# A sequence layer with ten dense experts on 8 cores: half of the pre-pass products on GpSimd, small filler matmuls, and other slots for the weights

## The reference, cut to what matters

```python
x = x + attn(layernorm(x))          # attn: state-space scan, then a 1024-4096-1024 MLP
x = x + ffn(layernorm(x))           # ffn: 2 shared experts and 8 routed ones
...
def step(s, u_t):                   # scan over time, 1024 channels x 16 states
    s = s * dA + u_t[..., None] * dB
    y = jnp.einsum('bdn,dn->bd', s, C_ssm)
    return (s, y)
...
h = gelu(rmsnorm(x) @ w1 + b1) @ w2 + b2
...
h_s = experts(u, W1_s, W2_s).sum(-2)            # every token, 2 experts
scores = sigmoid(u @ centroids); top 2 of 8
h_r = sum of gk * experts(u, W1_r, W2_r) over the top 2
return u + h_s + h_r
```

## Time and profile before

| what | us |
|---|---|
| two executions | 7874.85 and 8011.66 |
| their median | 7943.26 |
| the profiled execution, its own time | 7874.85 |
| span of its slowest core (core 1), the one shown | 7872.9 |
| spans of all cores | 7825.0 to 7872.9 |
| start and first load | 0 to 87 |
| pre-pass | 87 to 592 |
| scan | 592 to 2105 |
| MLP | 2105 to 2660 |
| router | 2660 to 2900 |
| experts and output | 2900 to 7873 |

### The profile page before, as it was taken

The page is one execution under the profiler, slowest core; times in us unless marked ns, Lnnn a source line. Parts: engine busy times, 40 slices in busy tenths (PEclk is TensorE's granted clock), DMA queues, the critical chain, the costliest instruction groups (busy, mean ns, idle before and its releaser), DMA issues.

```text
span 7872.9 us, 63136 instructions; the slowest of 8 cores (7825.0 to 7872.9 us)
## 1 busy us (share of the span) xinstructions
PE 5210.4 (66%) x23040; PEld 2278.9 (29%) x23040; DVE 2353.5 (30%) x2813; ACT 1454.9 (18%) x2046; POOL 1666.4 (21%) x1608
## 2 busy tenths in 40 slices
PE   0000000000288527999999999999999999999998
PEld 0000000000133213444434444444444444444443
DVE  5889898989611350000000000000000000000001
ACT  5780000000111002211122111222111221111220
POOL 0007786967300001101111111111011111111110
PEclk5555555555699768999999999999999999999997
DMA  3100000000133105555555555555555555555553
GB/s 94 27 0 0 6 0 6 0 8 0 14 46 50 23 11 89 70 67 70 74 87 73 67 70 75 68 74 67 70 70 75 72 71 68 70 71 73 70 73 78
DMA packets 555731, 412.68 MB, mean 52 GB/s; under 512 B 13194, under 2 KB 546586, under 8 KB 553764
## 3 DMA queue, kind: packets, MB, share of 16 engines
q0 software_dynamic: 545280, 381.73, 36.3%
q1 hardware_dynamic: 7844, 18.54, 0.7%
q10 hardware_dynamic: 2304, 8.39, 0.3%
HBM read 765.12 MB, written 12.58 MB: 99 GB/s over the span
## 4 chain that ended last, share of the span: by engine, by line
PE 60%; issue 13%; DVE 13%; DMA 7%; POOL 5%; ACT 2%; DVEq 0%; POOLq 0%; SPq 0%; ACTq 0%
PE ps L939 29%; PE ps L900 23%; POOL SSb L266 5%; DMA STAT<-W1r 4%; PE ps L710 3%; DVE SSb L554 3%; PE ps L668 3%; DVE BIG L269 2%; DVE BIG L266 2%; DVE MXS L269 1%; DVE MXS L266 1%; PE ps L991 1%; DMA STAT<-W1s 1%; DMA WBUF<-W1r 1%; POOL SSb L273 1%
## 5 line engine op out<-in xcount | busy, mean ns | idle before, releaser
L939 PE MATMUL ps<-WBUF,XR 128*128 128x512 bf16 x10240 | 2262.2, 384 | 131.9 <-DVE BIG L269 111.4
L276 ACT ACTIVATE XR<-ps,BIA 128x512 bf16<-128x512 f32 x1280 | 879.4, 687 | 3791.0 <-PE ps L900 3791.0
L939 PEld LDWEIGHTS ps<-WBUF,XR 128*128 128x128 bf16 x10240 | 1010.1, 99 | 1384.1 <-issue 211.1
L269 DVE SCALAR_TENSOR_TENSOR BIG<-ps,WTOK,BIG 128x512 f32<-128x512 f32 x256 | 171.5, 744 | 3657.9 <-PE ps L939 3657.9
L900 PE MATMUL ps<-MXS,WBUF 128*128 128x512 bf16 x5120 | 1140.4, 380 | 95.2 <-DVE MXS L262 38.2
L900 PE MATMUL ps<-MXS,STAT 128*128 128x512 bf16 x5120 | 1137.3, 380 | 76.0 <-DMA STAT<-W1r 58.7
L419 PE MATMUL ps<-BIG,ONE 128*128 128x512 bf16 x32 | 13.9, 614 | 1432.1 <-ACT BIG L276 1432.1
L554 DVE TENSOR_TENSOR_SCAN SSb<-COEF,SSb,BIG 128x512 f32<-128x512 f32 x512 | 879.8, 1756 | 0.0
L900 PEld LDWEIGHTS ps<-MXS,WBUF 128*128 128x128 bf16 x5120 | 493.8, 98 | 729.8 <-issue 160.5
L900 PEld LDWEIGHTS ps<-MXS,STAT 128*128 128x128 bf16 x5120 | 494.2, 98 | 708.8 <-issue 137.5
L280 POOL DMA_DIRECT2D WBUF<-W2r x256 | 190.0, 746 | 1656.7 <-PE ps L939 1589.2
(11 more groups left out here) (88 smaller groups left out, 1820.6 us busy)
## 6 DMA issues: line engine op xcount, KB each, us to landing
WBUF<-W2r POOLq DMA_DIRECT2D x256, 512.0 KB, 5.5
WBUF<-W1r POOLq DMA_DIRECT2D x128, 512.0 KB, 6.2
STAT<-W1r POOLq DMA_DIRECT2D x128, 512.0 KB, 6.3
WBUF<-W2s POOLq DMA_DIRECT2D x64, 512.0 KB, 6.5
WBUF<-w POOLq DMA_DIRECT2D x40, 512.0 KB, 5.9
WBUF<-W1s POOLq DMA_DIRECT2D x32, 512.0 KB, 6.2
STAT<-W1s POOLq DMA_DIRECT2D x32, 512.0 KB, 6.4
XR<-x SPq DMA_DIRECT2D x1, 8192.0 KB, 35.9
```

Source lines behind the costliest of these rows:

```text
L269: return lambda e: e.scalar_tensor_tensor(out, in0, s, in1, op0, op1, accum_out=acc)
L276: return lambda e: e.activation(out, in0, fn, bias=bias, scale=scale, accum_out=acc)
L939: last = e.matmul(ps[tgl * 2 + ti][:, 0:TT], haps[ti][:, tgl * 128:(tgl + 1) * 128], w2t, start=(hsub == 0), stop=(hsub == NH - 1))
```

## The change

It does five things.

1. In the pre-pass the even gn stay as they were. For the odd gn POOL multiplies the weight row with the input into `prod_p` (one buffer of 512 columns, region `ss_tmp`, the same columns as `tmp_p`), and DVE sums `prod_p` by a `tensor_scalar` with an accumulator output.
2. `pe_warm` puts a matmul of 128x128x128 of ones into ps3 on PE's list, after every even gn in the pre-pass and in the scan (64 a tile, 512 in all). It waits for the DVE instruction emitted last, and nothing waits for it.
3. The two W1 slots are now both in STAT (columns 0 to 1023 and 1024 to 2047), and W2 has four slots in WBUF, `% 4`. `w2slot2` is defined and not used.
4. The load of the first w1 chunk in advance is gone; it is emitted at the start of the MLP like the others.
5. The router's bf16 tile names one more region of WBUF among its writes.

```diff
+        def pe_warm():
+            b.plan["t"].append((
+                [("v", b.cnt["v"])],
+                lambda e: e.matmul(ps[3][:, 0:128], ONE[:, :], ONE[:, :],
+                                   start=True, stop=True), None, 0))
...
-        w1slot = [(WBUF[:, 3072:4096].bitcast(BF16), [wb_w1[1]]),
-                  (STAT[:, 0:1024].bitcast(BF16), [st_rg[0], st_rg[1]])]
+        w1slot = [(STAT[:, 0:1024].bitcast(BF16), [st_rg[0], st_rg[1]]),
+                  (STAT[:, 1024:2048].bitcast(BF16), [st_rg[2], st_rg[3]])]
         w2slot = [(WBUF[:, i * 1024:(i + 1) * 1024].bitcast(BF16),
-                   [[wb_w2[0], wb_w2[1], wb_w1[0]][i]])
-                  for i in range(3)]
+                   [[wb_w2[0], wb_w2[1], wb_w1[0], wb_w1[1]][i]])
+                  for i in range(4)]
...
+            prod_p = SSb[:, 4 * TT + 2 * GN:5 * TT + 2 * GN]
             for gn in range(GN):
...
-                b.op("v", STT(MXS[:, dumpo:dumpo + TT], ew, 1.0,
-                              up_ap[:, g * TT:(g + 1) * TT], ALU.mult,
-                              ALU.mult, acc=smp_ap[:, gn:gn + 1]),
-                     reads=[expw_rg[esl], up_rgs[g]],
-                     writes=dump_rg + [smp_rg[pt]])
+                if gn % 2 == 0:
+                    b.op("v", STT(MXS[:, dumpo:dumpo + TT], ew, 1.0,
+                                  up_ap[:, g * TT:(g + 1) * TT], ALU.mult,
+                                  ALU.mult, acc=smp_ap[:, gn:gn + 1]),
+                         reads=[expw_rg[esl], up_rgs[g]],
+                         writes=dump_rg + [smp_rg[pt]])
+                else:
+                    b.op("p", TTo(prod_p, ew, up_ap[:, g * TT:(g + 1) * TT],
+                                  ALU.mult),
+                         reads=[expw_rg[esl], up_rgs[g]], writes=[ss_tmp])
+                    b.op("v", TSc(MXS[:, dumpo:dumpo + TT], prod_p, 1.0,
+                                  None, ALU.mult, ALU.add,
+                                  acc=smp_ap[:, gn:gn + 1]),
+                         reads=[ss_tmp],
+                         writes=dump_rg + [smp_rg[pt]])
+                if gn % 2 == 0:
+                    pe_warm()
...
+                if gn % 2 == 0:
+                    pe_warm()
...
-            if t == NT - 2:
-                w1c0, w1rgs0 = w1slot[0]
-                b.dma("qg", DMA(w1c0.rearrange("p (dg h) -> p dg h", h=256),
...
-                if not (q == 0 and hc == 0):
...
-                        psl = (hsub // 4) % 3
+                        psl = (hsub // 4) % 4
...
-        xbf4_rgs = [wb_w2[0], wb_w2[1], wb_w1[0]]
+        xbf4_rgs = [wb_w2[0], wb_w2[1], wb_w1[0], wb_w1[1]]
...
-                    psl = (hsub // 4) % 3
+                    psl = (hsub // 4) % 4
```

More of the change, by code:

```diff
@@ L652, in build_program @@
                 h0 = q * QH + hc * 256
[L653 to L658 removed]
+                src = dr["w1"][:, h0:h0 + 256].rearrange(
+                    "(dg p) h -> p dg h", p=128)
+                b.dma("qg", DMA(w1c.rearrange("p (dg h) -> p dg h", h=256),
+                                src), writes=w1rgs)
                 for hs in range(2):
```

10 lines of the change are left out of this document (2 added, 8 removed).

## The result

| | us |
|---|---|
| changed kernel, 14 executions: median (lowest to highest) | 8722.64 (8277.31 to 8954.89) |
| kernel before in the same job, 12 executions | 8002.21 (7842.88 to 8772.06) |
| ratio of the counted executions | 1.0562 [1.0464, 1.0660] |
| the same two kernels on another chip, medians of all executions | 8261.43 against 7883.75 |
| ratio of the counted executions there | 1.0473 [1.0421, 1.0526] |

What is left to explain is a ratio of 1.047 to 1.056 where 1.044 was forecast.

The account below looks back on a forecast made before the run. The prediction took DVE to bound the first 2.1 ms (pre-pass and scan) and PE the rest. 7874.85 + 284 (loop) + 62 (tile changes) = 8221 us, +4.4%, range 8120 to 8310.

Parts of the forecast that it names:

- The ring of sum, multiply and product: Pre-pass loop: one product buffer makes sum, multiply and product follow one another, 2.72 us a pair against 1.61, +284 us.
- a bound at +26 us: Pre-pass loop: POOL-to-DVE hand-overs of 0.2 us in place of the assumed 0.1 would add 26 us.
- That product and multiply exclude each other: Pre-pass loop: POOL's product and DVE's even multiply do not overlap; the product ends 1.11 us after the multiply.
- beside the even multiply: Rival, pre-pass loop: the product overlaps the even multiply, pair 2.25 us, +164 us, total 8101 us; chance 0.08.
- The sum is the long form: Pre-pass loop: DVE's sum with accumulator takes 0.69 us; the short form, 0.43, would give back 67 us.
- Between the tiles: Four tile changes: the next load now stands behind the products, +15.4 us each, +62 us in all.
- Item 2, on the path up to the experts: 0: Small matmuls in pre-pass and scan cost 0; without the late load, each tile change would be 4.5 us longer.
- the rival asked for a lifted clock: Rival, pre-pass and scan: small matmuls raise PE's clock, saving 28 us and 2 at the MLP's start, total 8191; chance 0.06.
- Item 3 at 0: Experts: the new weight slots gain nothing, since PE waits for no W2 load and W1 keeps two slots.
- its bound of -72: Experts: -72 us if all of PE's waits for W1 loads, 58.7 and 13.4 us, went.
- Items 4 and 5 at 0: MLP start: the second W1 chunk still arrives some 23 us early, and the added wait is for finished readers; 0.
- the slowest core moves with the rest: Whole kernel: terms added to the profiled execution's 7874.85 us, with everything behind the pre-pass shifted and of the same length.

Follow-up runs that it names:

- one_input: `split_hoist` with the even gn on DVE as a one-operand sum of the weight row, input product left out; one execution, cores 7989 to 8011 us.
- scan_dve: Kernel before with the scan's odd-gn multiply and add moved from POOL to DVE; median 8134.27 us, lowest 7669.93, no ratio.
- two_buf: `split_hoist` with two product buffers in turn instead of one; 7926.08 us in the counted execution of two.
- split_hoist: Kernel before plus item 1, with the next tile's bf16 load issued ahead of the products; 8398.86 us, ratio 1.0367 [1.0033, 1.0701].
- split_only: Kernel before plus item 1 alone (odd products on POOL, one product buffer); 8264.86 us, ratio 1.0431 [1.0230, 1.0633].
- warm_dense: `warm_only` with 12 small matmuls in place of one at every even gn; 7893.28 us in the counted execution of two.
- warm_only: Kernel before plus item 2 alone, the 512 small matmuls in pre-pass and scan; 8205.24 us, no counted execution, no ratio.
- slots_only: Kernel before plus items 3, 4 and 5 alone (weight slots, no load in advance); 7964.69 us, ratio 0.9996 [0.9938, 1.0055].
- best: Kernel before with items 3, 4 and 5, the scan without POOL, and the scan of gn + 1 emitted ahead; 7573.86 us, ratio 0.9607 [0.9583, 0.9631].
- after_again: The changed kernel, unaltered, run again on the same chip as `nowarm`; 8261.43 us, ratio 1.0473.
- nowarm: Changed kernel without its 512 small matmuls (item 2 undone); single counted execution 8231.56 us, 1.045 over the kernel before's mean, no interval.
- warm_pre: Kernel before plus the 256 small matmuls of the pre-pass only; ratio 1.0162 [1.0097, 1.0228].
- warm_scan: Kernel before plus the 256 small matmuls of the scan only; ratio 1.0062 [1.0028, 1.0097].

## Why the prediction was wrong by its number and right about the pre-pass

**The ring of sum, multiply and product: right, its hand-over too short.** Forecast 0.81 + 0.69 + 1.11 + 0.10, measured 0.80 + 0.69 + 1.13 + 0.20. The hand-over was taken from gaps of 0.14 and 0.17 less "a little other work"; it is 0.20, the value that the prediction kept as a bound at +26 us. With 2.81 for 2.72 the loop costs 307 instead of 284. That product and multiply exclude each other was an inference from six lengths of the earlier trace rows; `one_input` shows it (with the open end named there), `scan_dve` shows it from the other side, and `two_buf` shows that the loss needed the one buffer as well: 2.81 with one, mostly 1.7 to 1.8 with two. The rival "beside the even multiply" was wrong in the premise, not in its arithmetic: where the exclusion is taken away (`one_input`), the pair is 2.30, and that rival had 2.25.

**The sum is the long form: right.** 0.69 with its read-out, an instruction named TENSOR_SCALAR_CACHE_REDUCE in the trace. The rule of the Trainium skill, "SBUF — State Buffer", Who interferes with whom, that `tensor_scalar` can enter a two-port mode but not the form that also writes out its accumulator, agrees with the 686 ns here against the 427 of the earlier trace rows; that the mode is what makes the short form short, no run here shows.

**Between the tiles: right in place, 13.5 for 15.4.** From the issue of the load to the first matmul it is 8.31 us, not the 9.93 of the earlier trace rows. 54 us instead of 62; `split_hoist` gets 60 back. Loop and changes together 361, measured 352 to 359 at the start of the scan, forecast 346: the loop was 23 us too short and the changes of tile 8 too long, and that these nearly cancel is luck.

**Item 2, on the path up to the experts: 0, right with the late load, and 20 us without it, 18 as priced.** On the clock: the rival asked for a lifted clock. One matmul a pair leaves 0.51 in the scan and on core 3 also in the pre-pass; core 1 had 0.62 there, and its matmuls at the change of tile still took 3.57. Cores 1 and then 3 of the changed kernel, and core 6 of `split_only`, which has no small matmul at all:

```profile
87.00:960.00 873.00, 95.70 (x320) 34.70 (x319) 427.98 (x1085) 389.31 (x528) 459.41 (x261) 0.62 0.04 9
...
87.00:960.00 873.00, 95.69 (x320) 34.91 (x320) 427.81 (x1084) 389.46 (x528) 460.27 (x261) 0.51 0.05 10
...
87.00:960.00 873.00, 28.33 (x63) 8.25 (x64) 428.79 (x1081) 387.25 (x525) 456.93 (x260) 0.86 0.04 8
```

So the 0.62 is no work of the small matmuls: `split_only` shows 0.86 on a core that has none, and there, too, eight matmuls at a change of tile take 3.57 us.

The rule weighed there (the Trainium skill, "TensorE: Matmul & The Clock Gate", What's actually happening) agrees with the pre-pass of `warm_dense`, where the clock did rise to 0.89. Even then the experts start only some 6 us earlier than in `warm_only`.

**Item 3 at 0: right, as far as the runs can tell.** `slots_only` has a ratio of 0.9996 and a middle core of 7830 against 7826, and the sum for `best` comes out without it. One reading of the prediction was short: its bound of -72, "if all those waits went", is the STAT row alone, and PE waited for the slot in WBUF too, 9.5 us on that core. **Items 4 and 5 at 0: right.** From the first scan to the experts it is 2366 to 2369 us on cores 0 to 3 of the changed kernel and 2365 to 2368 before.

**The sum against the result.** The prediction added 346 us to the kernel before. A middle core of the kernel before takes 7827 us, which makes 8173; the counted cores of the changed kernel have medians of 8175 in the first job and 8163 on the other chip. So for a core the sum was right within 10 us.

**The step that failed: the slowest core moves with the rest.** The prediction made its sum against 7874.85, the slowest core's time, and let that core's distance from the others stand; what lies behind the pre-pass was to be shifted "and of the same length", and item 2 was put at 0. In the kernel before the distance is about 30 us (7873 over a median of 7841 in the profiled execution). In the changed kernel it is 77 us on cores 0 to 3 of the first profiled execution (8250 over 8173) and 98 in `after_again` (8260 over 8162). That is 0.6 to 0.8% more for the slowest core, of which the sum had nothing; it takes the ratio of `after_again` from what a middle core lost, 8163 over 7833 or 4.2%, to its 4.7%. The first job's 1.056 holds more than that: in 8351.33 cores 4 to 7 end at 8246 to 8350, cores 4 and 5 at a granted clock of 0.806, and with two counted executions the rest of that ratio stays unexplained.

The extra distance comes in the experts, out of waits for W1 loads, in a stage that the forecast called untouched. In the kernel before this is seldom: 11 of 304 counted cores are late. In the kernels with small matmuls at one a pair it is 30 of 220: 17 of 96 in the changed kernel, 4 of 24 in `warm_only`, 9 of 100 in `warm_pre` and `warm_scan`. In `nowarm`, `split_only`, `split_hoist`, `slots_only` and the scan's kernels together it is 7 of 228 (`best` included); `two_buf` and `one_input` have 1 of 20. That speaks for item 2, to which the prediction gave 0. It is an association: the definition of late was made after the runs, the executions are few, the cores of one execution are not independent of each other, and the jobs ran on different chips. How 512 matmuls that end some 900 us before the experts should delay loads in them is not shown; `warm_dense` with twelve times as many had no late core in 12. On a middle core the same matmuls go with 30 us less in one job (`after_again` against `nowarm`) and 30 to 40 us more behind the pre-pass in another (`warm_pre`, `warm_scan`). The cause of the late cores stays open, and with it the size of item 2.

## What to carry to other kernels

Before work is moved from one engine to another, look in the trace for a place where both already run on operands of the same memory, and take the lengths from there: the product of this case took 1.26 us alone and 1.78 beside the multiply, and two engines sharing the work took 2.81 us a pair where one took 1.61. The same rows, read the other way, said that the scan was losing 0.5 us an instruction to POOL, and taking POOL out of it (with the scan of gn + 1 ahead, 3.9%) is worth more than anything else tried here. Take the length of a stage before from more than one execution: the one profiled here was 14 us long for a middle core, enough to make an edit that did nothing look like a gain. Forecast the slowest of eight cores as a core plus a distance of its own, and give that distance a range.

## What the runs showed of the hardware that was not expected

- **What DVE runs beside a POOL product decides its length.** A product of 512 columns with two SBUF operands takes 1.27 us beside a DVE instruction of 0.69 us with one SBUF operand, and 1.78 beside one of the same length with two (`one_input`, `split_hoist`). The two DVE instructions also differ in kind.
- **The hand-over from POOL to DVE is 0.20 us** (405.16 to 405.36). From DVE to POOL it is 0.14: the sum's read-out ends at 403.24 and the product, whose release it is, starts at 403.38.
- **A dependent DVE instruction costs 0.2 us.** With scan and STT in turn on DVE a gn takes 2.05 us when the STT reads the scan before it, and 1.84 when it reads the one before that.
- **The granted clock differs between cores on the same instructions**: 0.62 and 0.51 in the same stretch with the same 320 matmuls, and 0.50 to 0.86 among the cores of `split_only`, while the matmuls in these stretches keep the length of the lower level (eight in 3.57 us). With twelve small matmuls a pair it is 0.89 in the pre-pass, and eight matmuls take 1.89 us; the same twelve leave 0.51 in the scan.
- **One core in eight can lose 90 us to W1 loads.** Chunks of 6.9 us of matmuls hide a load on most cores; `after_again`'s core 4 loses 90 us in 320 chunks, 0.28 us on each, with loads that land 0.2 us later than on its neighbour.
